# Mixture-of-experts stage of a graph block on one core: routing and experts in one block, expert tiles in the order in which they fill

## The chip, the core and the metric

The program runs on one core of a Trainium2 chip. The metric is the time of one execution on the device in microseconds; before the change it is 2250.74 us, the median of 3 runs (2250.05 to 2253.19). The engines are TensorE (PE in the profile), VectorE (DVE), ScalarE (ACT), GpSimd (POOL) and SyncE (SP). The last two issue most of the DMAs here.

## The reference

There are 6250 nodes of 256 features. A layer norm, a graph attention and a linear attention with its feed-forward are added to x; they fill the first 1738 us and stay as they are. The change is in what follows, a mixture of six experts of which each node uses two:

```python
rh = relu(features @ router_w1 + router_b1)
expert_logits = softmax(rh @ router_w2 + router_b2)
top_w, top_i = top_k(expert_logits, 2)
routing_weights = softmax(top_w)
h1 = relu(features @ expert_w1[e] + expert_b1[e])
h2 = relu(h1 @ expert_w2[e] + expert_b2[e])
expert_out = h2 @ expert_w3[e] + expert_b3[e]
x = x + sum over the two chosen e of routing_weights * expert_out
```

Here features is the layer norm of the new x. Evaluated on its inputs, the reference sends 555, 560, 3178, 3152, 3953 and 1102 rows to the six experts; of them 294, 299, 1638, 1635, 2053 and 581 come from the first 3250 nodes.

## The kernel before, in words

The nodes are cut into 50 tiles (NT) of 125 rows (R). The graph attention leaves its sums in acc, 50 blocks of 258 numbers in the memory acc_mem (L162), and x in xn. Then come two blocks, each of which has a queue of instructions for every engine; a block ends when all its engines have ended.

**The routing block** (L1856). The 50 tiles go through in five groups (NS) of 6, 10, 10, 12 and 12 (SIZES). For each group ScalarE applies the relu of the graph attention (relus, L2045), VectorE adds it to xn (residual, L1926) and takes moments (L1932, L1935), and ScalarE writes the normed features (features, L2057) into pay3, a ring of three group buffers (PB3). TensorE transposes pairs of tiles (turn, L2108), multiplies by the router (router, L2118; logits, L2127), and ScalarE evacuates in between (turned, hidden). VectorE's route (L1964 to L2001) is a chain of some 35 small instructions: softmax, best two, the weights, and for each node its two row numbers. In it ScalarE is asked twice (the exponentials L2087 and L2089) and TensorE once (ranks, L2138 to L2142: prefix sums over nodes, on top of the counts cum of the groups before). GpSimd then writes each tile's rows (256 features, six weights, the node's number) into moe_rows in DRAM at those row numbers, with two indirect DMAs a tile (L1907). moe_rows has a region of REG rows for each expert. SP stores x to out as the base of the sum (L1866).

At the end TensorE counts the rows of each expert (L2159), and VectorE makes a table of 54 tiles (MT) of 256 rows (MR) from the counts (L2014 to L2035): the expert ej_i and the first row base_i of each, and the semaphore values clear1 and clear2 that VectorE waits for before it weighs a tile. SP fills the 256 rows behind the last one of each expert with blanks (L1876), which name no node.

**The expert block** (L2188). SP loads tile j (L2199) into a ring of six buffers, rowt. TensorE runs, for each j: up(j+1), mid(j), turn(j+2), down(j-1), with four matmuls in each (L2343, L2354, L2332, L2365; each has two records in the trace, since the numbers are f32). ScalarE evacuates the first three (L2300, L2309, L2292). VectorE runs, for each j: stage1(j+2) and stage2(j+1), which copy the weights of the expert of that tile (L2230, L2238), weighed(j-1), and stage3(j) (L2244 the third weights; L2249 the bias times the row's weight). weighed is the product of the result and the row's weight (L2268) into one of three buffers yo. GpSimd adds the 256 rows of a tile to out with two indirect DMAs (L2207). Two experts may add to the same node, so weighed(j) first waits for landed adds; this is decided by the table:

```python
V.tensor_tensor(change[:, 0, 1:MT], ej_f[:, 1:MT], ej_f[:, 0:MT - 1], ALU.not_equal)
V.scalar_tensor_tensor(clear1[:, 1:MT], change[:, 0, 1:MT], 32.0, gone[:, 0:MT - 1], ALU.mult, ALU.add)
```

Where the expert is that of tile j-1, the value asks only for the adds that were in that slot before; where it changes, 32 more, which are those of tile j-1 itself (clear2 does the same for tile j-2). With the counts above, the experts have 3, 3, 13, 13, 16 and 5 tiles, and tile 53 is an empty one.

## Time and profile before

| what | value |
|---|---|
| profiled execution, its own time | 2249.98 us |
| its span | 2248.2 us |
| median of the runs | 2250.74 us |
| PE busy | 1867.2 us, 83% |
| PE weight loads busy | 1504.5 us, 67% |
| DVE busy | 1667.0 us, 74% |
| ACT busy | 1443.1 us, 64% |
| POOL busy | 1199.3 us, 53% |
| L2207, adds to out (108) | 169.4 us, mean 1569 ns |
| L1907, scatters to moe_rows (100) | 99.6 us, mean 996 ns |
| L2343, L2354, L2365, matmuls of the experts (432 records each) | 104.1, 102.1 and 102.4 us |

Times in the trace count from the start of the span. A share of busy time is a mean over the whole span, and the change touches only the last 510 us of it, so the rows below are taken from stretches of that part. The name area stands for most of the on-chip buffers, acc_mem for the accumulators, bank for PSUM.

### The profile page before, as it was taken

What the parts mean: (1) busy time and instruction counts of PE and PEld (TensorE: products, weight loads), DVE (VectorE), ACT (ScalarE), POOL (GpSimd) and SP (SyncE); (2) the same over time, 40 slices, a digit from 0 to 9 for tenths busy, and PEclk for the clock granted to TensorE, in tenths of its full rate; (3) what the DMA queues carried; (4) which work ended last, traced back from release to release, by engine and by line L of the source; (5) the groups of instructions that cost most, each with busy time, mean ns of one, the idle gap of its engine ahead of it and who ended that gap; (6) DMA issues with size and microseconds to landing.
All of it is one profiled execution on the core that took longest, in us unless ns stands there. A gap on an engine that the chain in (4) does not pass through costs nothing. (4 is left out here: it accounts for less than half of the span.)

```text
span 2248.2 us, 49591 instructions
## 1 busy us (share of the span) xinstructions
PE 1867.2 (83%) x10102; PEld 1504.5 (67%) x10102; DVE 1667.0 (74%) x5284; ACT 1443.1 (64%) x4425; POOL 1199.3 (53%) x1169
## 2 busy tenths in 40 slices
PE   3788857699945999999999999999997671799996
PEld 2445435477734778778788787787786561688885
DVE  7888888877654888888888898988887642355553
ACT  5666568144303889889898898898987650333332
POOL 2010000056565777777777777777771377255554
PEclk9999978599756999999999999999999675899998
DMA  4321111021103444444444444444441543355553
GB/s 144 92 77 57 51 28 51 19 86 46 38 22 89 123 118 117 122 120 119 119 118 118 118 115 122 118 118 121 116 118 33 196 160 131 66 93 93 93 96 53
DMA packets 133895, 215.45 MB, mean 96 GB/s; under 512 B 42813, under 2 KB 89084, under 8 KB 133604
## 3 DMA queue, kind: packets, MB, share of 16 engines
q0 software_dynamic: 61920, 132.16, 24.4%
q1 hardware_dynamic: 67022, 72.68, 11.0%
q10 hardware_dynamic: 4662, 7.46, 1.1%
q8 instruction: 94, 1.54, 0.3%
q14 instruction: 197, 1.61, 0.2%
HBM read 150.28 MB, written 56.51 MB: 92 GB/s over the span
## 5 line engine op out<-in xcount | busy, mean ns | idle before, releaser
L1389 POOL DMA_INDIRECT area<-wh_table,area x788 | 769.2, 976 | 257.6 <-issue 235.3
L1716 PE MATMUL bank<-area 128*126 x1960 | 483.1, 389 | 27.9 <-ACT area L1636 14.7
L1716 PEld LDWEIGHTS bank<-area 128*126 128x126 f32 x1960 | 348.9, 188 | 100.7 <-issue 51.8
L1422 DVE TENSOR_SCALAR area<-iota_row,area 128x126 f32<-128x126 f32 x980 | 355.7, 370 | 25.8 <-ACT area L1589 17.4
L1622 ACT ACTIVATE area<-iota_row,area 128x126 f32<-128x126 f32 x735 | 285.9, 389 | 0.0
L2207 POOL DMA_INDIRECT out_dram<-area x108 | 169.4, 1569 | 163.5 <-DVE area L2268 146.8
L1636 ACT ACTIVATE area<-area 128x126 f32<-128x126 f32 x735 | 237.0, 386 | 0.4
L585 POOL DMA_INDIRECT sorted_slots<-area x112 | 134.9, 1204 | 118.9 <-DVE area L941 90.0
L1575 ACT ACTIVATE area<-bank 125x512 bf16<-125x512 f32 x245 | 145.5, 594 | 76.5 <-DVE area L1436 73.7
L1736 PE MATMUL bank<-area 128*128 128x250 f32 x800 | 188.4, 378 | 6.6 <-ACT area L1643 3.5
L1747 PE MATMUL bank<-area 128*125 128x256 f32 x800 | 188.9, 379 | 0.0
L1692 PE MATMUL bank<-ident,area 128*126 128x128 f32 x980 | 157.4, 284 | 36.5 <-DVE area L1422 36.5
L1497 DVE SCALAR_TENSOR_TENSOR acc_mem<-acc_mem,area,bank 125x258 f32 x245 | 117.7, 481 | 91.9 <-PE bank L1704 76.3
L1736 PEld LDWEIGHTS bank<-area 128*128 128x128 f32 x800 | 153.1, 192 | 26.7 <-ACT area L1643 3.9
L1436 DVE TENSOR_REDUCE area<-bank 125x1 f32<-125x512 f32 x245 | 167.4, 683 | 0.0
L1747 PEld LDWEIGHTS bank<-area 128*125 128x125 f32 x800 | 149.8, 187 | 23.2
L2268 DVE SCALAR_TENSOR_TENSOR area<-bank,area 128x256 f32<-128x256 f32 x108 | 47.4, 480 | 144.0 <-DMA out_dram<-area 76.3
L578 POOL IOTA acc_mem<- 128x788 f32 x1 | 0.8, 792 | 275.8 <-DVE area L850 275.8
L2300 ACT ACTIVATE area<-bank,area 128x256 f32<-128x256 f32 x108 | 45.4, 471 | 139.8 <-issue 133.6
L1907 POOL DMA_INDIRECT moe_rows<-area x100 | 99.6, 996 | 66.1 <-ACT area L2057 36.3
L1692 PEld LDWEIGHTS bank<-ident,area 128*126 128x126 f32 x980 | 103.7, 141 | 41.3 <-DVE area L1422 41.0
L2343 PE MATMUL bank<-area 128*128 128x256 f32 x432 | 104.1, 384 | 2.6 <-ACT area L2292 1.5
(410 smaller groups left out, 4049.6 us busy)
## 6 DMA issues: line engine op xcount, KB each, us to landing
area<-moe_rows SPq DMA_DIRECT2D x54, 264.0 KB, 2.8
area<-wh_table,area POOLq DMA_INDIRECT x788
area<-area SPq DMA_DIRECT2D x17, 388.5 KB
wh_table<-area SPq DMA_DIRECT2D x50, 126.5 KB
xn<-in_x_dram SPq DMA_DIRECT2D x25, 250.0 KB
xt_rows<-area SPq DMA_DIRECT2D x50, 125.0 KB, 2.5
area<-xt_rows SPq DMA_DIRECT2D x25, 250.0 KB
x_rows<-area SPq DMA_DIRECT2D x25, 250.0 KB
```

What stands on the lines that cost most here:

```text
L585: g.indirect_dma_start(out=slots[k % 2].rearrange("(a b) -> a b", b=1), out_offset=bass.IndirectOffsetOnAxis(ap=dest[:, j, k:k + 1], axis= ...
L1389: g.indirect_dma_start(out=gath[:, (i + GT) % RS, :], out_offset=None, in_=table, in_offset=bass.IndirectOffsetOnAxis(ap=idx_tab[:, i:i + ...
L1422: ins = V.tensor_scalar(xm[:, b, t, :], iota_row[:, :], rowl[:, j % 10, t:t + 1], fetched(j, D)[:, t:t + 1], ALU.is_equal, ALU.mult)
L1436: V.tensor_reduce(gmax[0:R, b:b + 1], bank[XT[j % 2]][0:R, :], AX.X, ALU.max).then_inc(d_m, 1)
L1575: A.activation(hot[0:R, b, :], bank[XT[j % 2]][0:R, :], ACT.Sign).then_inc(a_hot, 1)
L1622: last = A.activation(dist[:, t, :], iota_row[:, :], ACT.Abs, bias=rowl[:, j % 10, t:t + 1], scale=-1.0)
L1636: last = A.activation(sm[:, b, t, :], dist[:, t, :], ACT.Exp, bias=e3[:, b, t:t + 1], scale=-1.0e12)
L1692: last = T.transpose(bank[XT[j % 2]][0:RW, t * L:(t + 1) * L], xm[:, b, t, :], ident[:, :])
L1716: last = T.matmul(bank[US[b]][0:RW, 0:WROW], sm[:, b, t, :], gath[:, bass.ds(place + t, 1), 0:WROW].rearrange("p a w -> p (a w)"), start=( ...
L1736: last = T.matmul(bank[HB[p % 2]][:, i * CH:(i + 1) * CH], w_1[:, k, f * 128:(f + 1) * 128], x1T[:, k, :], start=(k == 0), stop=(k == 1))
L1747: last = T.matmul(bank[AB][0:R, r * D:(r + 1) * D], hT[:, f, r * R:(r + 1) * R], w_2[:, f, :], start=(f == 0), stop=(f == 7))
L2207: g.indirect_dma_start(out=out, out_offset=bass.IndirectOffsetOnAxis(ap=rowi[:, j % RB6, s, MW - 2:MW - 1], axis=0), in_=yo[:, j % 3, s, : ...
```

## The change

The two blocks become one. Each engine's queue holds its routing work and behind it, or in it, its expert work:

- **Payload.** pay3 is gone. acc_mem has 264 numbers a tile (MW) in place of 258 (WROW), and a tile's features, weights and node numbers are written where its sums were (pay). The row numbers posi have room for all 50 tiles, and the copies of the node numbers on GpSimd (L1900) and all waits for a free payload buffer are gone.
- **Table in two parts.** count(0) and table_of(0) come after group 2 and give the first 20 tiles (FULL): only whole tiles of 256 rows, from the rows of groups 0 to 2. table_of(0) stands in route(3), ahead of the wait for the ranks. table_of(1) gives the other 34 and stands behind stage3(1) in the expert loop. The order of tiles is: whole tiles of the early rows by expert, then the other whole tiles by expert, then one partly filled tile of each expert.
- **SP** loads tiles 0 to 19 when the scatters of groups 0 to 2 have landed and table_of(0) is done. Ahead of tile 20 it waits for table_of(1), writes the six blanks, and waits for them and for all late scatters. The ring has four buffers (RING3), and a load waits for d_wb of the tile four back in place of its landed adds.
- **GpSimd** writes groups 0 to 3 and three tiles of group 4 (AHEAD_OF_ADDS), then, for each j, the two adds of tile j and, for the first nine, the two scatters of one more tile of group 4.
- **VectorE** runs stage1(0), stage1(1) and stage2(0) ahead of route(4). stage3 copies the rows' weights (share) and the node numbers (node) out of the loaded tile.
- **ScalarE** does row_turned(0) and up(0) ahead of the exponentials of route(4), **TensorE** row_turn(0), up(0) and row_turn(1) ahead of ranks(4).
- PSUM banks are dealt out anew (TB2, H1, H2, YB, CN), and some scratch tiles lie in own_mem and iota_row.

The diff, cut to its core:

```diff
-OFF = 4 * 3 * 2 * ST
-RB6 = 6
+OFF = 4 * 2 * NT
+RING3 = 4
+EARLY = 3
+FULL = -(-(2 * R * sum(SIZES[:EARLY]) - NX * (MR - 1)) // MR)
...
-        acc_mem = sb("acc_mem", [128, (NT + 1) * WROW])
+        acc_mem = sb("acc_mem", [128, (NT + 1) * MW])
+        pay = acc_mem[:, :].rearrange("p (b w) -> p b w", w=MW)
...
+                for b in range(PB3):
+                    sp.wait_ge(sent[b], sent_rows[b])
+                sp.wait_ge(tabled, 1)
+                for j in range(MT):
+                    if j == FULL:
+                        sp.wait_ge(tabled, 2)
+                        for e in range(NX):
...
+                            sp.dma_start(moe_rows[bass.ds(b, MR), :].rearrange("(p s) c -> p s c", s=2), pair).then_inc(blanked, 16)
+                        sp.wait_ge(blanked, 16 * (NX + 1))
+                        sp.wait_ge(sent_late, 16 * 2 * sum(SIZES[EARLY:]))
...
+                    if j >= RING3:
+                        sp.wait_ge(d_wb, 2 * (j - RING3 + 1))
...
-                    g_.tensor_copy(payi3[0:R, b, 0:n, MW - 2:MW - 1], ids[0:R, f:f + n].unsqueeze(2)).then_inc(c3, 1)
...
+                for i in range(AHEAD_OF_ADDS):
+                    write(g, i, sent_late)
+                g_.wait_ge(base_out, 16 * NS)
+                for j in range(MT):
+                    g_.wait_ge(d_y, 2 * j + 2)
...
+                    if AHEAD_OF_ADDS + j < SIZES[g]:
+                        write(g, AHEAD_OF_ADDS + j, sent_late)
...
+                    step(V.tensor_tensor(cmp, iota_j[:, lo:hi].unsqueeze(2).to_broadcast(shape), seg_end[:, 0:n].unsqueeze(1).to_broadcast(shape), ALU.is_ge))
+                    step(V.tensor_tensor(cmp, cmp, seg_off[:, 0:n].unsqueeze(1).to_broadcast(shape), ALU.mult))
+                    step(V.tensor_reduce(both_f[:, lo:hi], cmp, AX.X, ALU.add))
...
+                    if g == EARLY:
+                        table_of(0)
                     dve.wait_ge(t_rank, g + 1)
...
                 def stage1(j):
+                    dve.wait_ge(tabled, 1 if j < FULL else 2)
...
                     dve.wait_ge(t_t, j + 1)
+                    V.tensor_copy(share[:, j % RING3, :, :], rowt[:, j % RING3, :, D:D + NX])
+                    step(V.tensor_copy(node[:, j % RING3, :], rowi[:, j % RING3, :, MW - 2]))
...
                     if j < MT:
                         stage3(j)
+                    if j == 1:
+                        table_of(1)
...
                     if g + 1 < NS:
                         root(g + 1)
+                    else:
+                        row_turned(0)
+                        up(0)
+                    act.wait_ge(d_lm, g + 1)
+                    A.activation(pe_[0:R, 0:n], lm[0:R, 0:n], ACT.Exp).then_inc(a_pe, 1)
...
+                    if g + 1 == NS:
+                        row_turn(0)
+                        up(0)
+                        row_turn(1)
+                    ranks(g)
+                    if g + 1 == EARLY:
+                        count(0)
+                count(1)
```

## Rows read from the trace of the kernel before

**Rows 1.** Windows: stretch, length, busy of PE, PEld, DVE, ACT, POOL, clock, DMA, GB/s
```profile
1876.00:1917.60 41.60, 0.00 (x0) 0.00 (x0) 0.00 (x0) 0.00 (x0) 23.71 (x26) 0.50 0.30 104
1917.60:2248.20 330.60, 307.41 (x1512) 268.92 (x1512) 154.07 (x486) 116.56 (x270) 169.41 (x108) 0.96 0.50 84
```
**Rows 2.** Timeline of PE at the joint: start, duration, instruction, idle before
```profile
1856.29 0.60 PE L2127 MATMUL bank<-area 128*125 128x6 f32 x4 [0.27 <-ACT area L2071]
...
1862.28 0.67 PE L2138 MATMUL bank<-area 125*125 125x72 f32 x2 [5.40 <-issue]
...
1867.31 0.68 PE L2142 MATMUL bank<-area,ones 125*125 125x72 f32 x2
...
1920.39 1.12 PE L2332 MATMUL bank<-ident,area 128*128 128x128 f32 x4 [50.40 <-DMA area<-moe_rows]
```
**Rows 3.** The chain that ended last, at the expert loop's start: start, us, what
```profile
1921.54 0.59 ACT area L2292
...
1922.27 3.77 PE bank L2343 x8
...
1926.12 0.84 ACT area L2300 x2
...
1927.65 1.96 PE bank L2343 x8
1929.61 1.73 PE bank L2354 x8
1931.34 0.44 PE bank L2332 x4
```
**Rows 4.** Timeline of POOL: last scatter of group 2, last of all, first add
```profile
1843.92 0.97 POOL L1907 DMA_INDIRECT moe_rows<-area  x1 [0.30 <-issue]
...
1906.02 0.97 POOL L1907 DMA_INDIRECT moe_rows<-area  x1 [0.30 <-issue]
1940.03 1.62 POOL L2207 DMA_INDIRECT out_dram<-area  x1 [33.04 <-DVE area L2268]
```
**Rows 5.** Timeline of DVE: route(4) and the table
```profile
1858.12 0.23 DVE L1968 TENSOR_REDUCE area<-area 125x12 f32<-125x72 f32 x1 [0.33 <-ACT area L2087]
...
1869.11 0.18 DVE L2001 CAST area<-area 125x24 int32<-125x24 f32 x1
1870.03 0.17 DVE L2014 TENSOR_TENSOR area<-bank,area 128x6 int32<-128x6 f32 x1 [0.75 <-PE bank L2159]
...
1872.31 0.50 DVE L2025 TENSOR_TENSOR area<-area 128x324 f32<-128x324 f32 x1
```
**Rows 6.** Timeline of DVE: weighings of tiles 5, 6, 46, 52 and 53
```profile
1967.12 0.88 DVE L2268 SCALAR_TENSOR_TENSOR area<-bank,area 128x256 f32<-128x256 f32 x2 [2.63 <-DMA out_dram<-area]
...
1973.54 0.88 DVE L2268 SCALAR_TENSOR_TENSOR area<-bank,area 128x256 f32<-128x256 f32 x2 [3.43 <-DMA out_dram<-area]
...
2197.50 0.88 DVE L2268 SCALAR_TENSOR_TENSOR area<-bank,area 128x256 f32<-128x256 f32 x2 [2.64 <-DMA out_dram<-area]
...
2228.73 0.88 DVE L2268 SCALAR_TENSOR_TENSOR area<-bank,area 128x256 f32<-128x256 f32 x2 [1.74 <-PE bank L2365]
...
2235.38 0.88 DVE L2268 SCALAR_TENSOR_TENSOR area<-bank,area 128x256 f32<-128x256 f32 x2 [4.76 <-DMA out_dram<-area]
```
**Rows 7.** Lines L1876 and L2199 on SP's queue: blanks, then loads of tiles
```profile
L1876 SPq DMA_DIRECT2D moe_rows<-area x6: 541/542/607, 1870.9 to 1877.5; - x6
...
DMA to landing us min/median/max: 3.1/3.3/3.5
...
DMA to landing us min/median/max: 2.5/2.8/3.5
```
**Rows 8.** Windows of PE: stretch, length, busy of PE, clock, DMA, GB/s
```profile
1856.00:1862.00 6.00, 0.61 (x5) 0.78 0.34 115
1862.00:1868.00 6.00, 5.71 (x26) 0.50 0.31 113
```

More of the change, by code:

```diff
@@ new lines, in gps_kernel @@
+        pay_i = acc_mem[:, :].bitcast(I32).rearrange("p (b w) -> p b w", w=MW)
+        rowt = take(RING3, 2, MW)
+        rowi = rowt.rearrange("p a b c -> p (a b c)").bitcast(I32).rearrange("p (a b c) -> p a b c", a=RING3, b=2)
+        share = take(RING3, 2, NX)
+        node = take(RING3 * 2).bitcast(I32).rearrange("p (a b) -> p a b", b=2)
+        s_x1, s_x2, s_x3 = (take(2, 2, D) for _ in range(3))
+        s_b1, s_b2 = take(2, 2), take(2, 2)
+        rowT = take(2, 2, MR)
+        h1, h2 = take(2, 2, MR), take(2, 2, MR)
@@ L1806, in gps_kernel @@
+        wb3 = take(2, D)
+        yo = take(3, 2, D)
+        take = carve(0, own_mem)
+        lg, lm, pe_, prob, p2, eq, iw, oh1 = (take(ST, NX) for _ in range(8))
+        take = carve(0, iota_row)
+        den = take(NT)
+        FT, RB, LG, PB, CN = (0, 1), (2, 3), (4, 5), 6, 7
+        TB2, H1, H2, YB = 0, (3, 2), (5, 1), (4, 6)
         w3_in = sem("w3_in")
@@ L1812, in gps_kernel @@
         d_va = sem("d_va")
-        a_lv = sem("a_lv")
         a_rs = sem("a_rs")
@@ L1912, in _ @@
+                for j in range(MT - PB3, MT):
+                    g_.wait_ge(sent[j % PB3], landed(j))
             @block.vector
@@ L2037, in _ @@
+                    route(g)
+                for j in range(MT + 1):
+                    if j + 2 < MT:
+                        stage1(j + 2)
+                    if j + 1 < MT:
+                        stage2(j + 1)
+                    if j > 0:
+                        weighed(j - 1)
+                    if j < MT:
+                        stage3(j)
+                    if j == 1:
+                        table_of(1)
             @block.scalar
@@ L2091, in _ @@
                         relus(g + 2)
+                row_turned(1)
+                for j in range(MT):
+                    if j + 1 < MT:
+                        up(j + 1)
+                    mid(j)
+                    if j + 2 < MT:
+                        row_turned(j + 2)
             @block.tensor
@@ L2327, in turn, with count, row_turn @@
+                def count(k):
+                    g = (EARLY, NS)[k]
+                    pe.wait_ge(d_cum, g)
+                    T.matmul(bank[CN][:, NX * k:NX * (k + 1)], ones[0:R, :], cum[0:R, g, :], start=True, stop=True).then_inc(t_cnt, 1)
+                def row_turn(j):
                     pe.wait_ge(row_in[j % 3], 16 * (j // 3 + 1))
```

440 lines of the change are left out of this document (198 added, 242 removed).

## The prediction

> **What bounds the kernel now.** I first read the busy time by stage. The last two blocks of the program are the routing block (1738 to 1917.6 us) and the expert block (1917.6 to 2248.2) [rows 1]. Nothing ahead of 1738 is edited apart from the pitch of an accumulator row, 264 numbers for 258, so the first 1738 us stand. In the expert block TensorE is busy 307 of 331 us at a granted clock of 0.96: it is the bound there, at one expert tile per (2197.50 - 1967.12) / 41 = 5.62 us (weighings of tiles 5 and 46) [rows 6]. In the joint between the blocks no engine computes: from 1876 to 1917.6 only GpSimd is busy, 23.7 of 41.6 us, and the clock is at its lower level, 0.50 [rows 1].
>
> The timeline of TensorE shows the size of the hole: its last group of ranks ends at 1868.0, and the first transpose of an expert tile starts at 1920.39, after 50.4 us of idleness [rows 2]. The timeline of GpSimd says why. It writes the rows of 50 node tiles in 100 scatters, one each 0.97 + 0.30 = 1.27 us; the last of group 2 goes out at 1843.92, and the 24 of group 3 and 24 of group 4 end at 1906.99 [rows 4]. The routing itself has its last row numbers at 1869.3 [rows 5]. Then there are some 10 us of end of block. So the expert loop waits for scatters, 48 of them from the last two groups, and for a block boundary, not for arithmetic.
>
> **The start of the expert loop.** I compare one instruction: the matmuls of up(1), the first of the steady loop, which start at 1927.65 [rows 3]. In the changed kernel SP starts to load when groups 0 to 2 have landed and the first table is written. The last scatter of group 2 goes out at 1843.9; with the 3 us that a transfer of rows needs [rows 7] that is 1847. The early table stands in route(3) where VectorE waits for ranks(3) (at full length about 4 us of small instructions beside 3.8 us of wait), so it is nearly free: group 3's scatters begin at most 0.5 us later. Tile 0 is in SBUF near 1851, ahead of its user: TensorE reaches row_turn(0) only behind the logits of group 4, which end at 1856.9 [rows 2].
>
> Ahead of route(4) the change puts a new chain: row_turn(0) 0.44, ScalarE's copy 0.59, up(0), ScalarE's relu 0.84 [rows 3]. ScalarE does them before the exponential for which route(4) waits, and behind that exponential wait VectorE, the ranks, and GpSimd's last scatters. From 1856.9, with up(0) at 1.73 to 1.9 us (the clock still high, as in the step at 1929.61 [rows 3]) and the small gaps between engines, the chain ends at 1861.1, the exponential at 1861.4 instead of 1858.1, where VectorE goes on behind it [rows 5]: 3.3 us. With the clock at half, up(0) takes 3.77 [rows 3] and it is 5.2. The ranks, 5.7 us at half clock [rows 2], then end at 1871.3, row numbers come 1.3 later as before, at 1872.6 [rows 5], the count takes 0.5, and up(1) starts at 1871.8. That is 55.85 earlier (bounds 53.6 to 57.6). Every DMA moved with it: GpSimd is through with group 3 at 1876.1 and with the first three tiles of group 4 at 1883.8, before the first adds, which come 12.4 us behind up(1) [rows 3, 4], at about 1886 with the ramp below; the base stores of x have long landed.
>
> **The clock on the way up.** Before, the half-clock steps of the start (up(0) 3.77 us) lay ahead of up(1) [rows 3]. Now TensorE enters up(1) out of the ranks, with the clock at 0.50 [rows 8]. In the trace the clock had risen some 7 us after the engine took up work at 1920.39 (the step at 1927.65 runs at full rate) [rows 2, 3]; the ranks begin at 1865.6, so I let it rise near 1875, and up(1) loses 1.7 us (0 to 3.5).
>
> **The late table.** It is queued on VectorE behind stage3(1), and behind it stand stage1(4), for which TensorE's up(4) waits. In the table before, 11 small instructions take from 1870.03 to 1872.31, 0.21 each, and one over 324 numbers 0.50 [rows 5]; that is about 0.17 and 1.0 ns a number. The new one has three over 34 x 18 = 612 (0.8 each) and some 18 small ones, 6.2 us. VectorE has about 1.8 us a tile to spare once share and node (0.45 us a tile, otherwise hidden) are added. Counting through: down(0) ends near 1884.4, weighing 0 and stage3(1) take until 1887.1, the table until 1893.3, and stage1(4) until 1893.9, where up(4) could have started at 1890.0: a stall of **3.9 us** (3.0 to 4.6).
>
> **GpSimd behind the adds.** Two adds take 2 x (1.6 + 0.3) = 3.7 us (the first one 1.62, with the 0.30 that stands before each instruction of a run) [rows 4]; for nine tiles two scatters are put behind them, 2.55 more. That makes 6.25 us a tile where TensorE gives 5.62. The late table puts weighing 1 at 1894.5; from its adds on GpSimd hardly pauses, and the adds of tiles 3 to 7 start at 1908.2 and then every 6.25 us; those of tile 7 have landed at 1938.4. Tile 8 is the first of expert 3, so its weighing waits for just that landing, while TensorE would be ready for it at 1933.3. Of 5.1 us, 2.2 are slack: between two downs TensorE has up, mid and a transpose, 2 x 1.73 + 0.44 = 3.9 us [rows 3], and in them VectorE starts the weighing (0.3 behind the down) and needs 0.9 for it and 0.4 for the weights of the next. With the wait behind the landing some **2.7 us** reach TensorE (0 to 5.6).
>
> **The blanks at tile 20.** SP writes six blanks (the last issued 6.6 us behind the first and landed 3.3 later [rows 7]) between the loads of tiles 19 and 20: with the first one's own 0.5, 10.4 us where the loads are 5.6 apart. The ring of 4 lets a load start when the tile four back is weighed with its bias (d_wb), some 6 us before its transpose; the load needs 2.8 [rows 7]. The rest stalls: **2.6 us** (0 to 5).
>
> **Changes of expert.** A weighing whose tile has another expert than the tile before waits for the adds before it. In the trace the interval is then 6.42 (1967.12 to 1973.54) and 6.65 (2228.73 to 2235.38) [rows 6]; I take 6.64, 1.0 above a tile. Alone it hides in the 2.2 us of slack. The reference's counts give 6 such changes before (tiles 3, 6, 19, 32, 48, 53), and 18 after: 1, 2, 8, 14, 22, 24, 25, 26, 32, 38, 45 and 47 to 53. The run 24 to 26 adds 0.8 (0 to 1.5). The run 47 to 53 sets the end: 7 x 6.64 = 46.5 from weighing 46 to weighing 53, where it is 2235.38 - 2197.50 = 37.9 now [rows 6]: **8.6 us** more (6.3 to 10).
>
> **The sum.** -55.85 + 1.7 + 3.9 + 2.7 + 2.6 + 0.8 + 8.6 = -35.5. The profiled execution took 2249.98, which makes 2214.4; the median of the runs, 2250.74, is 0.8 above it, so the forecast is **2215**.
>
> **A rule against the change.** Between 1856.9 and 1862.3 TensorE is idle for 5.4 us, and the granted clock goes from full by way of 0.78 to 0.50 [rows 2, 8]: from 2.4 to 1.2 GHz. The two stalls above of 2.6 to 3.9 us are shorter than any gap of this trace after which I saw it fall.
> The Trainium skill, "TensorE: Matmul & The Clock Gate", section "HAM oscillation — how this bites in real kernels", says that waits between bursts of matmuls put the engine back to its half rate, so that each next burst starts cold. The trace agrees for the gap of 5.4 us; for the shorter stalls of this sum no row shows it. By that rule the time is the second rival's.
>
> **The rivals.**
> - Forecast, 2215 (2208 to 2221 alone): chance 0.50.
> - The stalls disappear. GpSimd, SP and VectorE have more slack than I count, or they hide in one another (a stalled TensorE lets GpSimd catch up); only the late table and the tail remain: 2250.7 - 55.85 + 1.7 + 3.0 + 7 = 2206.5. For it: three of my terms have 0 as a bound. Chance 0.18.
> - The clock falls in the stalls at tiles 4, 8 and 20. Each then costs what the start shows, 7 us at half rate of which half is lost, 3.5 us; against it, a slow TensorE lets GpSimd catch up. Two such make 2222. Chance 0.16.
> - GpSimd is the bound of the first nine tiles. A scatter that costs beside VectorE's work what an add does (1.6 for 0.97 us [rows 4]) makes a tile 3.7 + 3.8 = 7.5 us, 6 us more by tile 8: 2221, and later landings up to 2226. Against it: VectorE is busy 154 of 331 us in this block [rows 1]. Chance 0.11.
> - Slower: half rate for good. A tile costs 11.24 us at half clock; the gain of 35.5 us is gone when 6.3 tiles run so, and with 10 the time is 2271. Place: each of the 18 changes of expert, should the adds land so late that TensorE idles at every one. It decides from 2.2 us of extra landing time. Against it: the changes in this trace cost 0.8 to 1.0 and left TensorE busy 307 of 331 us [rows 1, 6]. Chance 0.03.
> - The change doesn't do what it says: the early tiles start no sooner than all scatters have landed, and only the boundary's 8 to 10 us go, against 8.6 in the tail and the stalls. About 2251. The wait asks for groups 0 to 2 alone, so 0.02.
>
> **How the numbers follow.** Two in ten outside: the range reaches from the second case (2205) to the upper end of the third and fourth (2226). A measurement of this kernel can tell 0.2%, 4.5 us. All cases but the last two are faster by more: faster 0.95; the last is split with the slower one: same 0.02, slower 0.03.
>
> **What would show each step right or wrong.** The first expert matmuls near 1858 and up(1) near 1872 (if later than 1880, the start is wrong); an idle time of TensorE of 3 to 5 us ahead of up(4), released by VectorE; GpSimd without a pause from tile 3 to 8, then VectorE released by the landing of adds at tile 8; a gap of 2 to 3 us at the transpose of tile 20, released by the load; weighings 6.6 us apart in the last seven tiles; the granted clock at 1.00 in the loop apart from its first 5 us. The forecast is wrong if ranks(4) wait for up(0) much longer than 3.3 us, if the clock falls in the stalls, or if the first 1738 us move.

## The result, and the profile after

The changed kernel takes 2228.82 us (median of 4 runs, 2221.72 to 2232.24) against 2251.97 us of the kernel before in the same comparison (2250.05 to 2253.91): a ratio of 0.989 (95% interval 0.987 to 0.992). Its profiled execution took 2228.68 us with a span of 2226.9. It is faster by 23 us, where the forecast said 35.5, and 2.8 us above the upper end of the range.

In the profiles of this case the start of the routing block (ScalarE's first table load in it) lies anywhere from 1729.6 to 1744.8 us, although the instructions ahead of it are the same in all changed kernels. So I compare, in the profiled executions, the stretch from there to the last weighing: 1738.37 to 2235.38 = 497.0 us before, 1738.08 to 2214.69 = **476.6 us** after. The lead of the changed kernel, counted from the start of the routing block, tells where the time went. Weighing j is the step in which VectorE weighs tile j:

| reached | lead forecast, us | lead measured, us |
|---|---|---|
| up(1) | 55.85 | 56.6 |
| weighing 0 (behind the clock's ramp) | 54.15 | 54.0 |
| weighing 4 (behind the late table) | 50.25 | 46.7 |
| weighing 9 (behind GpSimd's queue) | 47.55 | 40.7 |
| weighing 20 (behind the blanks) | 44.95 | 34.4 |
| weighing 46 (behind the changes 22 to 26) | 44.15 | 30.6 |
| weighing 53, the last | 35.5 | 20.4 |

The start came as forecast. All of the five losses behind it are larger. The windows (columns as in [rows 1]) show the joint filled, and an expert loop that is not at its full clock:

```profile
1876.00:1917.60 41.60, 36.30 (x167) 30.85 (x166) 21.62 (x78) 12.96 (x30) 27.14 (x23) 0.92 0.48 104
1917.60:2226.90 309.30, 274.31 (x1321) 235.65 (x1318) 153.82 (x523) 101.13 (x234) 168.04 (x110) 0.95 0.49 88
```

TensorE is busy 36.3 of the 41.6 us in which it stood still before [rows 1], and 274 of 309 us behind that, 89%, where it was 307 of 331, 93%. The timeline of TensorE at the start answers [rows 2, 3]: row_turn(0), up(0), the ranks, up(1), mid(0).

```profile
1856.24 0.63 PE L2345 MATMUL bank<-ident,area 128*128 128x128 f32 x4
1857.64 1.97 PE L2356 MATMUL bank<-area 128*128 128x256 f32 x8 [0.77 <-ACT area L2233]
...
1864.93 0.66 PE L2327 MATMUL bank<-area 125*125 125x72 f32 x2 [4.89 <-issue]
...
1869.96 0.67 PE L2331 MATMUL bank<-area,ones 125*125 125x72 f32 x2
...
1870.81 3.76 PE L2356 MATMUL bank<-area 128*128 128x256 f32 x8
1874.36 2.68 PE L2367 MATMUL bank<-area 128*128 128x256 f32 x8
```

up(0) still runs at full rate (1.97 us), the ranks start 2.65 us later than in [rows 2], and up(1) pays with the half rate (3.76 us for 1.96 [rows 3]). Further on the same timeline has the stalls, at up(4), down(7), the transposes of tile 20 and the downs of the last tiles:

```profile
1894.28 3.78 PE L2356 MATMUL bank<-area 128*128 128x256 f32 x8 [4.22 <-DVE area L2125]
1897.85 2.88 PE L2367 MATMUL bank<-area 128*128 128x256 f32 x8
...
1944.39 3.57 PE L2380 MATMUL bank<-area 128*128 128x256 f32 x8 [3.81 <-DVE area L2139]
...
1995.62 1.11 PE L2345 MATMUL bank<-ident,area 128*128 128x128 f32 x4 [4.79 <-DMA area<-moe_rows]
1996.53 3.03 PE L2380 MATMUL bank<-area 128*128 128x256 f32 x8
...
2202.35 2.58 PE L2380 MATMUL bank<-area 128*128 128x256 f32 x8 [2.87 <-DVE area L2139]
2209.18 3.78 PE L2380 MATMUL bank<-area 128*128 128x256 f32 x8 [4.25 <-DVE area L2139]
```

The idle times in brackets are 3.8 to 4.8 us at the first three, and each is followed by matmuls of 3 to 3.8 us for 1.9. The windows show the granted clock (the column ahead of the last two):

```profile
1890.00:1892.00 2.00, 0.05 (x1) 0.00 (x0) 1.83 (x7) 0.00 (x0) 1.64 (x2) 1.00 0.87 140
1892.00:1894.00 2.00, 0.00 (x0) 0.00 (x0) 1.17 (x7) 0.00 (x0) 0.39 (x1) 0.75 0.20 72
1894.00:1898.00 4.00, 3.72 (x9) 3.01 (x10) 3.30 (x12) 0.00 (x0) 1.62 (x1) 0.50 0.00 0
...
1944.00:1948.00 4.00, 3.61 (x9) 2.95 (x10) 2.29 (x10) 0.00 (x0) 3.42 (x2) 0.57 0.49 100
...
1996.00:1998.00 2.00, 2.00 (x8) 1.73 (x7) 0.00 (x0) 0.59 (x1) 0.00 (x0) 0.50 0.06 22
```

So the clock goes from its upper level, 2.4 GHz, to the lower one, 1.2 GHz, in or at the end of each of the first three stalls. What VectorE does there answers [rows 5, 6]: the late table begins, its first instruction over 612 numbers, stage1(4) behind it, then the weighings of tiles 8, 46, 47, 48 and 53.

```profile
1886.78 0.15 DVE L2041 TENSOR_TENSOR area<-bank,area 128x6 int32<-128x6 f32 x1
...
1888.60 0.80 DVE L2052 TENSOR_TENSOR area<-area 128x612 f32<-128x612 f32 x1
...
1893.79 0.43 DVE L2125 COPY area<-area 128x512 f32 x1
...
1943.12 0.88 DVE L2165 SCALAR_TENSOR_TENSOR area<-bank,area 128x256 f32<-128x256 f32 x2 [8.31 <-DMA out_dram<-area]
...
2166.61 0.88 DVE L2165 SCALAR_TENSOR_TENSOR area<-bank,area 128x256 f32<-128x256 f32 x2 [1.07 <-DMA out_dram<-area]
...
2175.03 0.88 DVE L2165 SCALAR_TENSOR_TENSOR area<-bank,area 128x256 f32<-128x256 f32 x2 [4.94 <-DMA out_dram<-area]
...
2181.32 0.88 DVE L2165 SCALAR_TENSOR_TENSOR area<-bank,area 128x256 f32<-128x256 f32 x2 [2.81 <-DMA out_dram<-area]
...
2214.69 0.88 DVE L2165 SCALAR_TENSOR_TENSOR area<-bank,area 128x256 f32<-128x256 f32 x2 [4.20 <-DMA out_dram<-area]
```

GpSimd's timeline answers [rows 4]: the two adds of tile 2, the two scatters behind them, the first add of tile 3, and the first add of tile 7. All but the first have only the 0.30 us that stand before every instruction of a run:

```profile
1904.38 1.62 POOL L1970 DMA_INDIRECT out_dram<-area  x1 [2.11 <-DVE area L2165]
1906.30 1.79 POOL L1970 DMA_INDIRECT out_dram<-area  x1 [0.30 <-issue]
1908.39 0.99 POOL L1950 DMA_INDIRECT moe_rows<-acc_mem,area  x1 [0.30 <-issue]
1909.69 1.21 POOL L1950 DMA_INDIRECT moe_rows<-acc_mem,area  x1 [0.30 <-issue]
1911.21 1.62 POOL L1970 DMA_INDIRECT out_dram<-area  x1 [0.30 <-issue]
...
1937.26 1.62 POOL L1970 DMA_INDIRECT out_dram<-area  x1 [0.30 <-issue]
```

And SP's queue around tile 20 answers [rows 7]: load(19), the six blanks, load(20).

```profile
1980.59 0.33 SPq L1927 DMA_DIRECT2D area<-moe_rows  x1
1981.67 7.41 SPq L1918 DMA_DIRECT2D moe_rows<-acc_mem  x6
1992.45 1.59 SPq L1927 DMA_DIRECT2D area<-moe_rows  x2
```

### The profile page after: what moved, and what is told of

Same layout as the page of the kernel before. It is cut to its first block and busy times, and to the rows that moved or that the text cites. A ratio compares the mean times of both kernels' runs of the same rounds, so it can differ in the third digit from the quotient of the medians.

```text
span 2226.9 us, 49705 instructions
## 1 busy us (share of the span) xinstructions
PE 1877.5 (84%) x10104; PEld 1508.4 (68%) x10104; DVE 1689.4 (76%) x5415; ACT 1442.7 (65%) x4425; POOL 1200.0 (54%) x1164
## 5 line engine op out<-in xcount | busy, mean ns | idle before, releaser
L1721 PE MATMUL bank<-area 128*126 x1960 | 483.1, 389 | 30.0 <-ACT area L1641 15.1
L1427 DVE TENSOR_SCALAR area<-iota_row,area 128x126 f32<-128x126 f32 x980 | 354.5, 369 | 24.8 <-ACT area L1594 17.1
L1950 POOL DMA_INDIRECT moe_rows<-acc_mem,area x100 | 100.6, 1006 | 66.9 <-ACT acc_mem L2213 36.6
L1697 PEld LDWEIGHTS bank<-ident,area 128*126 128x126 f32 x980 | 103.8, 141 | 39.8 <-DVE area L1427 39.5
L2380 PE MATMUL bank<-area 128*128 128x256 f32 x432 | 108.4, 395 | 16.3 <-DVE area L2139 16.3
```

The lines of the kernel that those rows point to most:

```text
L1427: ins = V.tensor_scalar(xm[:, b, t, :], iota_row[:, :], rowl[:, j % 10, t:t + 1], fetched(j, D)[:, t:t + 1], ALU.is_equal, ALU.mult)
L1697: last = T.transpose(bank[XT[j % 2]][0:RW, t * L:(t + 1) * L], xm[:, b, t, :], ident[:, :])
L1721: last = T.matmul(bank[US[b]][0:RW, 0:WROW], sm[:, b, t, :], gath[:, bass.ds(place + t, 1), 0:WROW].rearrange("p a w -> p (a w)"), start=( ...
L2380: last = T.matmul(bank[YB[j % 2]][:, s * D:(s + 1) * D], h2[:, j % 2, k, s * 128:(s + 1) * 128], s_x3[:, j % 2, k, :], start=(k == 0), sto ...
```

## The experiments

All are edits of the changed kernel. The table has the lead over the kernel before at some weighings (w4 is weighing 4), the stretch from the start of the routing block to the last weighing in the profiled execution, and the measured time (median and ratio to the kernel before with its 95% interval; one run each for 5 and 10). From the start of the routing block to weighing 0 they differ only in where the late table stands and in two scatters, and it takes 146.1 to 147.4 us; so 1.3 us in the stretch tell nothing. The single times carry the spread of the first 1738 us as well, and tell less.

Each stretch is one profiled execution, and the part behind weighing 20 spreads more. All kernels with three segments run the same instructions there, and of their lead they lose from w20 to w53 14.0 us (changed), 17.1 (1), 14.4 (2), 13.5 (4), 13.9 (5), 13.7 (6), 16.1 (10) and 16.8 (12); those with two segments lose 1.0 to 1.5. So for the kernels with three segments a difference of 3 us in the stretch isn't shown to come from the edit, and the lead at w20 tells more.

| kernel | w4 | w9 | w15 | w20 | w32 | w46 | w53 | stretch | time, us | ratio |
|---|---|---|---|---|---|---|---|---|---|---|
| changed | 46.7 | 40.7 | 40.8 | 34.4 | 31.4 | 30.6 | 20.4 | 476.6 | 2228.8 | 0.989 (0.987 to 0.992) |
| 1 late table sooner | 51.2 | 43.3 | 42.2 | 35.0 | 29.1 | 28.4 | 17.9 | 479.1 | 2223.5 | 0.989 (0.985 to 0.993) |
| 2 blanks spread | 47.1 | 41.0 | 41.0 | 41.4 | 37.8 | 37.2 | 27.0 | 470.1 | 2220.7 | 0.988 (0.985 to 0.992) |
| 3 two segments | 47.9 | 41.3 | 40.3 | 34.0 | 34.4 | 33.0 | 32.7 | 464.3 | 2218.8 | 0.986 (0.983 to 0.990) |
| 4 busy, 16 matmuls | 46.3 | 40.7 | 40.6 | 33.7 | 30.4 | 29.9 | 20.2 | 476.8 | 2228.0 | 0.991 (0.988 to 0.994) |
| 5 busy, 9 matmuls | 48.9 | 41.0 | 40.7 | 34.2 | 30.7 | 30.1 | 20.3 | 476.7 | 2235.1 | |
| 6 scatters thin | 46.7 | 45.8 | 39.5 | 32.1 | 28.3 | 28.2 | 18.4 | 478.6 | 2232.6 | 0.991 (0.988 to 0.994) |
| 7 = 1 + 2 + 3 | 52.3 | 44.5 | 44.5 | 44.7 | 45.3 | 43.8 | 43.7 | 453.3 | 2199.9 | 0.977 (0.975 to 0.980) |
| 8 = 7 + 6 | 51.8 | 50.7 | 44.4 | 44.0 | 44.4 | 42.9 | 42.6 | 454.4 | 2209.5 | 0.981 (0.978 to 0.984) |
| 9 = 7 + scatters even | 52.6 | 51.5 | 49.7 | 49.8 | 50.3 | 48.8 | 48.6 | 448.4 | 2198.9 | 0.978 (0.975 to 0.980) |
| 10 scatters even | 46.6 | 45.8 | 44.6 | 37.6 | 31.9 | 31.7 | 21.5 | 475.5 | 2223.0 | |
| 11 = 7 + one scatter | 51.7 | 50.8 | 51.0 | 51.1 | 51.5 | 50.1 | 49.6 | 447.4 | 2197.6 | 0.975 (0.974 to 0.977) |
| 12 one scatter | 47.0 | 46.2 | 46.8 | 38.8 | 32.8 | 32.1 | 22.0 | 475.0 | 2222.8 | 0.986 (0.984 to 0.988) |

**Experiment 1: the late table one tile sooner**, so that VectorE has written it before stage1(4) is due.

```diff
-                    if j == 1:
+                    if j == 0:
                         table_of(1)
```

> One edit to the changed kernel: table_of(1) stands behind stage3(0) in place of stage3(1), where VectorE was idle from 1874.8 to 1884.6 us apart from two small stages. Theory A (a stall of TensorE costs its idle time and then a stretch at half rate): the 4.2 us of idleness ahead of up(4) go, and with them the 2.8 us that up(4) and mid(3) lose at half rate, together 7.0; the adds of the first tiles start without a pause, so GpSimd falls further behind and the wait at tile 8 grows by 1 to 3 us. Net 4 to 6 us faster than the changed kernel, a median near 2224, the granted clock at 1.00 from 1880 to 1940. Theory B (the missing gain sits in slower landings of transfers, stalls are mere idle time that something else fills): at most 2 us faster, near 2227.

The stall ahead of up(4) and its half rate are gone: the lead at weighing 4 is 4.5 us larger. At weighing 9 it is 2.6, at weighing 20 only 0.6. The median, 2223.5, is the 2224 of theory A, but no gain is shown: the profiled execution reached the routing block 8.5 us sooner than that of the changed kernel, and the ratio to the kernel before is 0.989 for both. The timeline of TensorE shows where it went, to the wait at tile 8, which grew from 3.81 to 5.39 us:

```profile
1933.03 3.78 PE L2380 MATMUL bank<-area 128*128 128x256 f32 x8 [5.39 <-DVE area L2139]
```

GpSimd's queue is the same length, so tiles that come sooner wait longer at the change. Another 2.9 us go between tiles 20 and 32, mostly at the change to tile 26 (8.45 us for 7.4), with an idle time of 2.52 us and a half rate (3.45) behind it. The adds waited for there landed late (3.9 us behind the end of the second one for 2.8), as they did at other tiles in experiments 10 and 12; that the edit caused it isn't shown.

**Experiment 2: the blanks one by one**, each ahead of the load of one of tiles 10 to 15, which is free to do: they follow the counts alone, and the late table is out by then.

```diff
-                    if j == FULL:
-                        for e in range(NX):
-                            sp.reg_load(ends[e % 2], blank_i[0:1, e:e + 1])
+                    if 10 <= j < 10 + NX:
+                        e = j - 10
+                        sp.reg_load(ends[e % 2], blank_i[0:1, e:e + 1])
```

> One edit to the changed kernel: SP issues the six blanks one by one behind the loads of tiles 9 to 14, and only waits for them ahead of tile 20. Theory A (six issues of 1.2 us each and their landing stand in a row between two loads): the 4.8 us of idleness at the transpose of tile 20 and the 1.5 us of half rate behind it go: 6.3 us faster than the changed kernel, near 2222.5, no idle time of TensorE at the load of tile 20. Rival (the ring of four buffers is too short by itself): an idle time stays there, 2 us or more, and the gain is below 3.

The idle time at tile 20 is gone, with its half rate, and the lead at weighing 20 is 41.4 us for 34.4. All but 0.4 of it lasts to the end: 6.5 us. The blanks' term is real, and nothing behind it takes it back.

**Experiment 3: two segments for three.** Each expert's last, unfilled tile goes with its other late tiles, instead of all of these tiles at the end. 12 changes of expert are left of 18.

```diff
-        SEG = 3 * NX
+        SEG = 2 * NX
...
-                        step(V.scalar_tensor_tensor(fulls[:, SEG:SEG + NX], odd6, 1.0, whole, ALU.min, ALU.add))
+                        step(V.scalar_tensor_tensor(whole, odd6, 1.0, whole, ALU.min, ALU.add))
```

> One edit to the changed kernel: the partly filled tile of each expert comes right behind its late whole tiles (two segments by expert in place of three), so there are 12 changes of expert in place of 18, and in the last seven tiles there are two (50 and 53) in place of seven. Theory A (each change costs about 1.0 to 1.4 us more than a tile, hidden only when alone): weighing 46 to 53 takes 48.1 us now and should take 7 x 5.63 less the early end of TensorE, some 39, so 9 faster; two of the three changes at 24 to 26 are apart as well, 2 more, and the table has 408 numbers in place of 612, 0.6: 10 to 12 us faster than the changed kernel, near 2217. Rival (the last tiles are slow because they are the last, their adds have nothing beside them to hide behind): at most 4 us faster.

12.3 us come back. The weighings 46 and 53 of this run (timeline of DVE):

```profile
2170.49 0.88 DVE L2165 SCALAR_TENSOR_TENSOR area<-bank,area 128x256 f32<-128x256 f32 x2 [1.87 <-DMA out_dram<-area]
...
2208.66 0.88 DVE L2165 SCALAR_TENSOR_TENSOR area<-bank,area 128x256 f32<-128x256 f32 x2 [4.39 <-DMA out_dram<-area]
```

38.2 us for 48.1 in the changed kernel, and 37.9 before [rows 6]: 9.9 us of the tail were the seven changes in a row, and the rest came from the changes 24 to 26.

**Experiment 4: TensorE kept busy in the stall at up(4)** with 16 matmuls that nobody reads, once VectorE has read the counts out of the same bank.

```diff
+                    if j == 4:
+                        pe.wait_ge(z3, 6)
+                        for i in range(16):
+                            T.matmul(bank[CN][:, 256:512], ident[:, :], w_x1[:, i % 2, :], start=True, stop=True)
```

> The changed kernel with one addition: ahead of up(4), once VectorE has read the counts for the late table, TensorE runs 16 matmuls (some 3.8 us at full rate) whose result nobody reads, so that it is busy in most of the 4.2 us for which it waits there. I compare the stretch from the start of the routing block (ScalarE's first table load at 1738) to the last weighing, 476.6 us in the changed kernel. Theory A (the clock fell because TensorE idled): up(4) and mid(3) run at full rate, 1.9 and 1.9 us for 3.78 and 2.88, so the interval from weighing 1 to weighing 3 is 2.5 to 2.9 us shorter, and the granted clock stays at 1.00 from 1890 to 1900. The stretch comes to 474 us, if what is won is not taken back by GpSimd's adds behind it; then it is 476. Theory B (the clock fell for another reason, as the load of all engines at that moment): up(4) takes over 3 us again and nothing is won.

The clock stays at 1.00 from 1884 to 1902, and up(4) and mid(3) take 1.89 us each, as theory A said. But the 16 matmuls took 7.07 us, not 3.8 (each has two records in the trace, and I had taken records for matmuls), and outlasted VectorE's stage1(4) by 2.6 us, about what the clock gave. Nothing is won.

**Experiment 5: the same with 9 matmuls.**

```diff
-                        for i in range(16):
+                        for i in range(9):
```

> The changed kernel with 9 matmuls without use ahead of up(4) for 16. These matmuls have one operand in 32-bit numbers and took 0.44 us each, 7.07 us for 16, so that they outlasted the wait for VectorE by 2.8 us; nine take 4.0 us. Theory A (the half rate comes from TensorE's idleness and nothing else): up(4) starts at most 0.7 us behind VectorE's copy and takes 1.9 us, mid(3) too, the three intervals from weighing 0 to weighing 3 sum to 21.4 us rather than 24.2, and the stretch is 474 us (473 to 475). Theory B: up(4) takes over 3 us.

The timeline of TensorE: the nine, then up(4) and mid(3).

```profile
1896.77 4.05 PE L2355 MATMUL bank<-area,ident 128*128 128x256 f32 x18
1901.15 2.00 PE L2362 MATMUL bank<-area 128*128 128x256 f32 x8 [0.34 <-DVE area L2127]
1902.99 1.89 PE L2373 MATMUL bank<-area 128*128 128x256 f32 x8
```

2.00 us for 3.78: it is the idleness that took the clock, since nothing else was changed. The tiles up to 4 run 2.2 us sooner (the three intervals from weighing 0 to weighing 3 sum to 22.2 us, for 21.4 forecast and 24.2 before the edit). But at weighing 9 the lead is 41.0 for 40.7, and the stretch is 476.7, not 474: the second half of the forecast was wrong. Weighings 7 and 8 (timeline of DVE) tell why:

```profile
1935.52 0.88 DVE L2167 SCALAR_TENSOR_TENSOR area<-bank,area 128x256 f32<-128x256 f32 x2 [1.65 <-PE bank L2386]
...
1948.97 0.88 DVE L2167 SCALAR_TENSOR_TENSOR area<-bank,area 128x256 f32<-128x256 f32 x2 [9.99 <-DMA out_dram<-area]
```

VectorE waits 9.99 us there for 8.31. As in experiment 1, the time won ahead of tile 8 is spent in waiting for GpSimd. The traces show how fixed that wait is. In all seven kernels with the two scatters behind each tile (changed, 1 to 5 and 7) weighing 8 comes 38.4 to 38.8 us behind the first add of tile 2, and GpSimd pauses nowhere between; with the scatters thinner (6, 8 to 12) it comes 32.6 to 34.3 us behind. So what reaches tile 8 is only how much sooner tile 2 is weighed: 2.5 us in experiment 1, 0.3 here.

**Experiment 6: group 4's late scatters thinner at first**, one behind the adds of each of tiles 0 to 7 and two behind those of tiles 8 to 12.

```diff
-                    if AHEAD_OF_ADDS + j < SIZES[g]:
-                        write(g, AHEAD_OF_ADDS + j, sent_late)
+                    for m in ([j] if j < 8 else range(2 * j - 8, 2 * j - 6)):
+                        if AHEAD_OF_ADDS + m // 2 < SIZES[g]:
+                            write(g, AHEAD_OF_ADDS + m // 2, sent_late, (m % 2,))
```

> The changed kernel with group 4's late scatters spread otherwise: one behind the adds of each of tiles 0 to 7 and two behind those of tiles 8 to 12, instead of two behind each of tiles 0 to 8. Theory A (GpSimd is behind at tile 8, because two adds and two scatters take it 6.4 to 6.7 us a tile): the adds come with the tiles, 5.6 us apart or after short pauses, the interval from weighing 7 to weighing 8 falls from 11.7 to 6 or 7 us, the idle time of 3.8 us at down(8) and its half rate go, and the stretch from the start of the routing block to the last weighing goes from 476.6 to 471 us (469.5 to 473). Theory B (what is waited for at tile 8 is the time that the adds take to land, whatever was queued): the interval stays at 10 us or more and less than 2 us is won.

Theory A is right at tile 8: the interval is 7.3 us, the adds of tile 7 begin 1.16 us behind their weighing (5.90 in the changed kernel), and the idle time is gone. But the stretch is 478.6, 7.6 above what it said: the stall stands at tile 14 now, the next change of expert, behind the tiles with two scatters. Weighings 13 and 14:

```profile
1967.50 0.88 DVE L2166 SCALAR_TENSOR_TENSOR area<-bank,area 128x256 f32<-128x256 f32 x2 [1.46 <-PE bank L2381]
1980.46 0.88 DVE L2166 SCALAR_TENSOR_TENSOR area<-bank,area 128x256 f32<-128x256 f32 x2 [9.05 <-DMA out_dram<-area]
```

13.0 us for 7.0. At tile 8 the landing takes 2.4 us behind the end of the second add in both kernels. So the landing is not what is long there; the queue ahead of it is, wherever a change comes behind a run of pairs.

**Experiment 7: 1, 2 and 3 together.**

> The edits of three earlier runs together: the late table behind stage3(0), the six blanks one ahead of each of the loads of tiles 10 to 15, and two segments for three. If their effects on the stretch from the start of the routing block to the last weighing (476.6 in the changed kernel; +2.5, -6.5, -12.2 with one alone) add up, it is 460 us. If the table's move is worth more once the tiles behind it have fewer changes, 456 to 458. Tile 8 should still show its wait for the landing of the adds, with 4 us of idleness and a half rate.

The stretch is 453.3 us, below both forecasts. The single effects are +2.5, -6.5 and -12.3, -16.3 in all; together they make -23.3. If the blanks and the segments keep their single effects (the two were not run without the table's move), that move, worth nothing alone, brings 4.5 here: of what it wins at tile 4 tile 8 takes a part again, but no change behind that does. Tile 8 still has its 5.38 us of idleness.

**Experiment 8: 7 with the scatters of experiment 6.**

> As the run before, with group 4's late scatters spread thin as well. Theory A (the table, GpSimd's queue at tile 8, the blanks and the segments account for all of the loss behind up(1)): no idle time of TensorE over 2 us behind up(1) and a clock of 1.00 in every stretch behind the first 10 us. The stretch is then 497.0 - 56.8 + 2.5 for the ramp + 2 for the changes of expert that are left = 445 us (443 to 449), the median 2197 us. Rival: GpSimd or the landing of the adds is late again elsewhere (the stalls only move): 450 us or more, with waits of over 3 us at other changes of expert.

Theory A failed as in experiment 6 and the rival holds: 6.2 us are won at tile 8 and lost at tile 14, where TensorE idles for 5.32 us and then runs at half rate (3.78).

**Experiment 9: 7 with the scatters spread evenly.**

```diff
+                    for m in range(*[j + sum(j > k for k in (8, 9, 14)) for j in (j, j + 1)]):
```

> The early table, the blanks ahead of the loads of tiles 10 to 15, two segments for three, and group 4's 18 late scatters spread so that none are queued ahead of a change of expert: one behind the adds of tiles 0 to 7, two behind tiles 8 and 9, one behind tiles 10 to 13, two behind tile 14. With two behind each of tiles 8 to 12 the stall had moved from tile 8 (13.3 us from weighing 7 to 8, 7.8 after) to tile 14 (7.0 us, 13.2 after). Theory A (it is GpSimd's queue at a change of expert that costs, and the scatters fit between changes): the intervals into tile 8 and tile 14 are both under 8 us, there is no idle time of TensorE over 2 us behind up(1) up to tile 47, and the stretch from the start of the routing block to the last weighing is 454.4 - 6.2 = 448 us (446 to 450), the median 2250 - 49 = 2201 or less (2192 to 2200 if the first 1738 us are as usual). Rival: the stall moves once more, to the load of tile 20, for which the last scatters must have landed: an idle time of over 3 us there and 452 us or more.

The stretch is 448.4 us, as theory A said, and the median 2198.9. One part of it was wrong: the interval into tile 14 is 9.7 us, not under 8, because the tiles behind the change at 8 come 4.8 us apart, and two scatters there put GpSimd behind once more (the adds of tile 13 begin 3.65 us behind their weighing).

**Experiment 10: those scatters alone.**

> The changed kernel with only the 18 late scatters spread as in the run before (one, or two behind tiles 8, 9 and 14). Theory A: the 5.7 us that tile 8 lost come back and do not go elsewhere: the interval into tile 8 is 7 to 8 us, that into tile 14 about 7, that into tile 20 still 12, and the stretch is 476.6 - 4.5 = 472 us (470.5 to 473.5). Theory B (a stall that goes at tile 8 always comes back at the next change, since the GpSimd work of the first twenty tiles is the bound): 476 us or more.

475.5 us, above the range of theory A and half a us short of theory B. 5.1 us are won at tile 9; of these 1.3 are gone at tile 15 (the adds of tile 13 begin 2.9 us behind their weighing, for 1.15), 0.6 more at tile 20, and 2.7 between tiles 20 and 32, where the adds of tile 21 landed 4.2 us behind the end of the second one for 2.3.

**Experiment 11: one scatter a tile.** Four node tiles of group 4 go out ahead of the adds for three, in 2.8 us for which GpSimd waits for weighing 0; then one scatter behind each of tiles 0 to 13 and two behind tile 14.

```diff
-AHEAD_OF_ADDS = 3
+AHEAD_OF_ADDS = 4
...
+                    for m in range(*[j + (j > 14) for j in (j, j + 1)]):
```

> Early table, spread blanks and two segments, as before, but of group 4 four node tiles go out ahead of the first adds for three (GpSimd idles 2.8 us there, which holds the two scatters of 1.28 us), and the other 16 scatters follow one behind the adds of each of tiles 0 to 13 and two behind tile 14. In the run with two behind tiles 8 and 9 the adds of tile 13 began 3.65 us behind their weighing instead of 1.15, and the interval into tile 14 was 9.7 us. Theory A (GpSimd's queue: behind the change at tile 8 the tiles come 4.8 us apart, and two scatters there put it behind): the adds of tile 13 begin under 1.6 us behind their weighing, the interval into tile 14 is 7.0 to 7.4, and the stretch from the start of the routing block to the last weighing is 448.4 - 2.5 = 446 us (444.5 to 447). Rival: the two scatters more ahead of the adds delay adds(0) and give it back at tiles 1 and 2: 448 or more.

The weighings of tiles 7, 8, 13 and 14 (timeline of DVE):

```profile
1928.74 0.88 DVE L2168 SCALAR_TENSOR_TENSOR area<-bank,area 128x256 f32<-128x256 f32 x2 [2.23 <-PE bank L2383]
1936.29 0.88 DVE L2168 SCALAR_TENSOR_TENSOR area<-bank,area 128x256 f32<-128x256 f32 x2 [4.06 <-DMA out_dram<-area]
...
1962.56 0.88 DVE L2168 SCALAR_TENSOR_TENSOR area<-bank,area 128x256 f32<-128x256 f32 x2 [1.86 <-PE bank L2383]
1970.21 0.88 DVE L2168 SCALAR_TENSOR_TENSOR area<-bank,area 128x256 f32<-128x256 f32 x2 [4.15 <-DMA out_dram<-area]
```

7.55 and 7.65 us, with GpSimd on time (1.16 us) at both. Behind up(2) TensorE has no idle time above 1.6 us, and its clock is 0.98 to the end. The stretch is 447.4, 29.2 us below the changed kernel's (0.4 above the range of theory A: at tile 14 the adds took 3.05 us to land, for 2.4 in the changed kernel). The median of 2197.6 us is the lowest of all, 31 us below the changed one; against the kernel before it is 2.5% faster. The times alone don't separate it from experiments 7 and 9 (ratios of 0.977 and 0.978, with intervals that overlap).

**Experiment 12: that schedule alone.**

> The changed kernel with that schedule of the scatters alone (late table, blanks and three segments as they are). With two behind tiles 8, 9 and 14 alone the stretch was 475.5 rather than the 472 expected: 1.8 us were lost at tile 14 to GpSimd's queue, 1.9 at tile 22 and 0.7 at tile 32 to adds that landed later (4.2 us for 2.3 at tile 22). Theory A (the landings are chance, GpSimd's queue is the cause): the interval into tile 8 is 7 to 7.5, that into tile 14 7.0, that into tile 22 7.0, and the stretch is 472 us (471 to 473). Theory B (a tile 8 that starts sooner is always paid for behind it, by the landings among other things): 475 us or more again.

At tile 15 the lead is 46.8 us, 6.0 more than in the changed kernel: that is what GpSimd's queue costs, and theory A is right so far (7.3, 7.0). At tile 20 it is 4.4, at tile 32 1.4, at the end 1.6. So the sum is theory B's 475. 1.6 us go at the transpose of tile 20, where the blanks still stand (that transpose lies between weighings 16 and 17, an interval of 13.5 us for 12.2). Another 1.8 stand at tile 22, weighings 21 and 22:

```profile
2018.03 0.88 DVE L2166 SCALAR_TENSOR_TENSOR area<-bank,area 128x256 f32<-128x256 f32 x2 [2.15 <-PE bank L2381]
2026.76 0.88 DVE L2166 SCALAR_TENSOR_TENSOR area<-bank,area 128x256 f32<-128x256 f32 x2 [5.25 <-DMA out_dram<-area]
```

8.7 us for 6.9: the adds of tile 21 land 4.16 us behind the end of the second one for 2.34. Experiment 10 has 8.8 us at the same tile, the other kernels about 7, experiment 11 with the same scatters among them. What makes these adds land late stays open, and with it whether a tile 8 that starts sooner is always paid for, as theory B has it: at tile 20 the lead is still 4.4 us larger.

## Why the prediction was right and where it was wrong

**Right: the direction, the start and the places.** up(1) started at 1870.81 (1871.8 forecast), 56.8 us sooner (56.6 from the start of the routing block); up(0) at 1857.64 and at full rate; the exponential was delayed by 2.6 us (3.3). The late table took 6.2 us and its large instructions 0.80 each, as counted. There was an idle time ahead of up(4) released by VectorE, GpSimd without a pause from tile 3 to tile 7, the wait for the landing at tile 8, the gap at tile 20 released by its load, and the long tail. No loss appeared at a place that the prediction didn't name.

**Wrong: the stalls were priced as if the clock stayed up.** This is the first step of the prediction that failed. "The two stalls above of 2.6 to 3.9 us are shorter than any gap of this trace after which I saw it fall" was true of the trace and no evidence that the clock would hold. At up(4) and mid(3) 1.9 + 1.0 = 2.9 us were lost to the half rate, at down(7) 1.7, at tile 20 0.5 + 1.1 = 1.6: 6.2 us in all (each the duration of the slow groups less 1.9 or 0.6). Experiment 5 shows the cause: with TensorE busy in the same stretch, up(4) takes 2.00 us. It also shows that the 2.9 us at up(4) and mid(3) are lost at that place and not at the end, since 0.3 us of them are left at weighing 9.
The Trainium skill, "TensorE: Matmul & The Clock Gate", section "HAM oscillation — how this bites in real kernels", says that waits between bursts make each next burst start cold. By that rule, the trace agrees: after each of the stalls of 3.8 to 4.8 us the next group ran at half rate.

The second rival, which had this mechanism at 2222 us, was nearer than the forecast, but it took 3.5 us for each stall, where the rows show 1.6 to 2.9. What put the time above it are the sizes of the stalls themselves.

**Wrong: the sizes.** The terms that were mis-sized, the clock's share taken off. This is an account by place, from one trace, and not what a repair would bring:
- The ramp: 2.55 us for 1.7. mid(0) too ran at half rate in part (2.68).
- The late table: 4.4 for 3.9, within its bounds.
- GpSimd's queue: 4.4 for 2.7. From the adds of tile 2 to those of tile 7 it took (1937.26 - 1904.38) / 5 = 6.58 us a tile, where I counted 6.25. The scatters were not slower (0.98 to 1.2, so the third rival's 1.6 is wrong), but the adds are 1.6 to 1.8 each.
- The blanks: 4.7 for 2.6. From load(19) to load(20) it is 1992.45 - 1980.59 = 11.9 us for 10.4: the first blank is 1.1 behind the load for 0.5, the six take 7.4 to the end of the last one for 6.6, and the load needs 3.2 to land for 2.8.
- The changes: 3.85 for 0.8 from weighing 20 to 46 (3.0 of it by weighing 32, behind the changes 22 to 26), and 10.2 for 8.6 in the tail. I took 6.64 us for the interval at a change on the strength of two of the six in the trace before, 6.42 and 6.65. Three of the others stand there at 6.85, 6.81 and 6.85; by them the 7.0 to 7.4 at 24 to 26 would have been nearer. With three changes in a row there is nothing to hide the excess in, and 0.55 us each count in full. In the tail one interval of 8.4 (46 to 47) made the difference; the other six are 6.6 in the mean.

With the start 0.7 better, that is 0.7 - 0.85 - 6.2 - 0.5 - 1.7 - 2.1 - 3.05 - 1.6 = -15.3, against the -15.1 that the lead is short of the forecast.

**Wrong in kind: the terms don't add.** The sum took the late table and GpSimd's queue as two costs, one behind the other. Experiments 1 and 5 show that they overlap: take 4.5 or 2.2 us off at tile 4, and 2.6 or 0.3 are left at tile 9. GpSimd sets the time at tile 8 from the adds of tile 2 on. The prediction let the table delay up(4); what counts behind it is that it delays weighings 1 and 2. With GpSimd's queue short (experiment 11 beside 12) the 4.7 us of the earlier table, which is also shorter with two segments, are still 4.6 at tile 9. Each stall hides part of another, so that edits worth +2.5, -6.5, -12.3 and -1.6 us alone are worth -29.2 together. About half of the 11.3 us between these sums rests on the late landings behind tile 20 in experiments 1 and 12, whose cause is open. At weighing 20, ahead of them, the four alone bring 0.6, 7.0, -0.4 and 4.4, 11.6 in all, and together 16.7.

**Where the start's gain went**, then: of 54.0 us at weighing 0, 20.4 are left. 12.3 went into changes of expert that experiment 3 removes, 6.5 into the blanks with their half rate (2), some 10 into the late table and GpSimd's queue (what is left of experiment 11's 29.2 when the other two are taken off), and 4.4 are missing in experiment 11 still. The sum had 9.4, 2.6 and 6.6 for the first three.

## What to carry to other kernels

When idle time at a joint is filled, price every new stall of the busy engine twice, its length and the matmuls behind it at half rate, and then ask whether another engine's queue hides both. For an engine that is near its limit, add up its whole queue up to each point where someone waits for it, not its rate alone: small work should be queued in its pauses and never in the run ahead of a wait. And test repairs together as well as alone: the early table brought 0.6 us at weighing 20 alone, and with GpSimd on time its 4.7 us at tile 4 were still 4.6 at tile 9.

## What the runs showed of the hardware that I had not expected

- Short idle times can cost TensorE its clock. After 3.8 to 5.5 us the next group of four matmuls took 3.57 to 3.78 us in the changed kernel and experiments 1 and 5, after 2.52 us (experiment 1) 3.45 and after 2.87 (the changed kernel) 2.58; after 1.59 and 1.78 us (experiment 9) it took 2.00. But the length doesn't decide it: after 3.10 us (experiment 1), 2.95 (5), 2.85 (4) and 2.83 (12) the same group took 2.00. Two groups of experiment 1 (timeline of TensorE), the shorter idle time ahead of the slower one:

```profile
2048.86 3.45 PE L2380 MATMUL bank<-area 128*128 128x256 f32 x8 [2.52 <-DVE area L2139]
...
2196.39 2.00 PE L2380 MATMUL bank<-area 128*128 128x256 f32 x8 [3.10 <-DVE area L2139]
```

What decides between them is open. The clock was back at 1.00 within some 6 us of work.
- The landing of the adds follows the rows in a tile. The DMA view from weighing 46 to 47, then that from weighing 47 to 48 (queue, packets, MB, share of the engines' time):

```profile
q0 software_dynamic: 435, 0.40, 42.6%
```

```profile
q0 software_dynamic: 288, 0.05, 8.6%
```

Tile 46 is a full one; its adds landed 3.85 us behind the end of the second one. Tile 47 is nearly empty (43 rows by the reference's counts); its adds took 1.72 us. So a change behind a nearly empty tile is cheap: 6.3 us behind the tiles of 43 and 48 rows, 6.6 to 6.9 behind those of 78 to 113, 6.9 to 8.4 behind full ones. Why the adds of tile 46 took 3.85 where those of other full tiles took 2.3 to 2.8 wasn't settled; it isn't chance, since they took 3.4 to 3.9 in every kernel with three segments.
- The 1738 us ahead of the routing block vary by 15 us between executions of the same instructions, the 146 us behind that by 1.3. A difference of a few us in the expert tiles could be read only with the first part left out.
